# A two-layer graph network, last stage: five of nine chunks get relu and residual by VectorE out of PSUM

## What is computed

```python
h = maximum(layernorm(x), 0)
x = x + relu(gcn(h, W, b, gamma, beta, src, dst))       # first layer: scatter over the edges
h = maximum(layernorm(x), 0)
agg = segment_sum(edge_attr, dst)                       # sums of edge attributes by node
m = relu(concat([h, agg, u]) @ W1 + b1)
m = relu(m @ W2 + b2)
out = x + m @ W3 + b3
```

## Time and profile before

| | us |
|---|---|
| median of 3 runs | 744.41 |
| the 3 runs | 744.41, 748.85, 740.71 |
| the profiled execution: time | 737.08 |
| the profiled execution: span of the rows | 735.3 |
| TensorE busy | 669.1 (91%) |
| VectorE busy | 569.5 (77%) |
| ScalarE busy | 456.4 (62%) |
| GpSimd busy | 147.9 (20%) |

### The profile page before, as it was taken

The page is one execution under the profiler, slowest core; times in us unless marked ns, Lnnn a source line. Parts: engine busy times, 40 slices in busy tenths (PEclk is TensorE's granted clock), DMA queues, the critical chain, the costliest instruction groups (busy, mean ns, idle before and its releaser), DMA issues. The chain is left out here.

```text
span 735.3 us, 21540 instructions
## 1 busy us (share of the span) xinstructions
PE 669.1 (91%) x9010; PEld 574.0 (78%) x9010; DVE 569.5 (77%) x1115; ACT 456.4 (62%) x811; POOL 147.9 (20%) x184
## 2 busy tenths in 40 slices
PE   0898764899999999999999999989999999998996
PEld 0766553688988888888888988979888888896554
DVE  5997985988888888888888888488888898845622
ACT  1563583666666666667766666376666766666862
POOL 3652851111111110111111111020000000003622
PEclk9997685999999999999999999999999999999999
DMA  6300710556555444445555555365555555660122
GB/s 154 115 1 3 260 38 2 216 216 216 216 216 203 178 180 176 177 174 199 214 214 214 214 214 195 140 219 210 177 180 182 208 214 214 214 171 5 42 59 76
DMA packets 64878, 119.75 MB, mean 163 GB/s; under 512 B 3077, under 2 KB 22739, under 8 KB 64807
## 3 DMA queue, kind: packets, MB, share of 16 engines
q1 hardware_dynamic: 64246, 117.89, 45.7%
q0 software_dynamic: 576, 1.12, 0.6%
HBM read 115.81 MB, written 4.03 MB: 163 GB/s over the span
## 5 line engine op out<-in xcount | busy, mean ns | idle before, releaser
L1562 PE MATMUL ps_product<-counts_sb,table_sb 128*128 128x240 f16 (+1 forms) x2646 | 408.7, 261 | 0.0
L1381 ACT CAST counts_sb<-ps_counts 128x588 f16<-128x588 f32 x524 | 335.9, 649 | 103.5 <-PE ps_counts L1552 59.3
L1552 PE MATMUL ps_counts<-key_hot,lo_hot 128*128 128x147 bf16 x2096 | 384.9, 232 | 15.1 <-DVE key_hot L1430 6.2
L1562 PEld LDWEIGHTS ps_product<-counts_sb,table_sb 128*128 128x128 f16 x2646 | 240.4, 97 | 8.1
L1552 PEld LDWEIGHTS ps_counts<-key_hot,lo_hot 128*128 128x128 bf16 x2096 | 198.2, 98 | 60.1 <-ACT counts_sb L1381 17.8
L1430 DVE TENSOR_TENSOR key_hot<-key,iota_key 128x1176 bf16<-128x1176 f16 x262 | 199.7, 762 | 0.0
L1425 DVE TENSOR_TENSOR lo_hot<-src_lo,iota_key 128x1024 bf16<-128x1024 f16 x262 | 180.8, 690 | 17.7 <-PE ps_counts L1552 12.6
L1365 POOL TENSOR_SCALAR place_hot<-iota_c,slot_now 128x96 f32<-128x96 f32 x81 | 60.3, 757 | 470.6 <-PE ps_place L1598 457.1
L1441 DVE TENSOR_TENSOR attr_hot<-rel,iota_w 128x640 f32<-128x640 int16 x81 | 66.9, 825 | 54.9 <-PE ps_sums L1572 54.9
L1572 PE MATMUL ps_sums<-attr,attr_hot 128*32 128x128 f32 x3240 | 95.6, 276 | 0.0
L1572 PEld LDWEIGHTS ps_sums<-attr,attr_hot 128*32 128x32 f32 x3240 | 88.1, 111 | 4.5 <-issue 4.1
(11 more groups left out here) (279 smaller groups left out, 536.3 us busy)
## 6 DMA issues: line engine op xcount, KB each, us to landing
attr<-in_edge_attr_dram SPq DMA_DIRECT2D x80, 1280.0 KB, 8.2
acc<-in_x_dram SPq DMA_DIRECT2D x4, 768.0 KB, 8.5
attr<-in_x_dram SPq DMA_DIRECT2D x12, 256.0 KB, 5.3
out_dram<-y_ring SPq DMA_DIRECT2D x12, 256.0 KB, 2.3
src_padded<-in_src_dram SPq DMA_DIRECT2D x1, 805.7 KB, 7.4
attr<-in_edge_attr_dram SPq DMA_DIRECT2D x2, 320.0 KB, 8.0
attr<-in_edge_attr_dram SPq DMA_DIRECT2D x1, 640.0 KB, 3.9
raw_d<-in_dst_dram SPq DMA_DIRECT2D x1, 540.0 KB
```

What stands on the lines that cost most here:

```text
L1381: act.copy(counts_sb[s % 2][:].rearrange("p h (n t) -> p h n t", n=WN) [:, :, :, k * QUAD:(k + 1) * QUAD], ps_counts[n % 2][:, :, 0:KEYS]. ...
L1552: ins = pe.matmul(ps_counts[quad % 2][:, c, 0:KEYS], lo_hot[:, held, pair, :, q % 2], key_hot[:, held, pair, :, q % 2], start=True, stop=True)
L1562: ins = pe.matmul(ps_product[side][:, 0:SLOTS] if tiles == TS else product, table_sb[:, h, low, :], counts_sb[side][:, h, :] if tiles == T ...
```

## The change

For the later chunks with an even number (4, 6, 8, 10 and 12) VectorE does, in a new function `join`, what ScalarE and GpSimd did: for each block one `scalar_tensor_tensor` out of `ps_turn[0]`, `dinv * sums + x` into `relu_ring[0]`, then, after waiting for the last of them, one `tensor_tensor` over the chunk that takes the maximum of that and `x`, into `xs`. That is relu and residual at once, as max(a + x, x) = relu(a) + x. `join(c)` stands in VectorE's slot of `TURNED_IN`, behind the copy h2t and ahead of the statistics of the slot before. The wait of chunk 12 for its loaded rows (`tail_in`) goes with it to VectorE.

The odd chunks (5, 7, 9 and 11) stay with ScalarE and GpSimd. They alone use `ps_turn[1]` and `relu_ring[1]` now, and the even ones bank and slot 0. So `turn_sums` waits for `joined` ahead of chunks 6, 8, 10 and 12, and for `relu_ready` ahead of 7, 9 and 11; the statistics and x3 of an even chunk wait for `joined` (`x1_is_ready`). Nothing else is changed, and the DMAs are the same.

```diff
--- before.py
+++ after.py
@@ -1680,16 +1680,23 @@
             ps_turn, ps_h2, ps_3 = ([bank(f"ps_{n}{k}", [P, NC], scope) for k in range(2)] for n in ("t", "h", "three"))
             ps_1, ps_2 = (bank(f"ps_{n}", [P, NC], scope) for n in ("one", "two"))
             (zeroed, b1u_done, b1u_ok, conv_turned, relu_ready, x1_ready, dve_step, var_ok, root_ok, norm_ok, h2_ready,
-             h2_turned, h2t_ready, m1_ready, z1_ready, m2_ready, z2_ready, m3_ready, x3_ready, y_ready, tail_in) = (
+             h2_turned, h2t_ready, m1_ready, z1_ready, m2_ready, z2_ready, m3_ready, x3_ready, y_ready, tail_in, joined) = (
                 sem(f"mlp_{n}", scope) for n in
                 "zeroed b1u_done b1u_ok conv_turned relu_ready x1_ready dve_step var_ok root_ok norm_ok h2_ready "
-                "h2_turned h2t_ready m1_ready z1_ready m2_ready z2_ready m3_ready x3_ready y_ready tail_in".split())
+                "h2_turned h2t_ready m1_ready z1_ready m2_ready z2_ready m3_ready x3_ready y_ready tail_in joined".split())
             y_out = [sem(f"y_out{k}", scope) for k in range(2)]
 
             def slot(buffers, c):
                 return buffers[:, c % 2, 0:width(c) * P]
 
 
+            def x1_is_ready(engine, c):
+                if c % 2:
+                    engine.wait_ge(x1_ready, (c - LEAD) // 2 + 1)
+                else:
+                    engine.wait_ge(joined, (c - LEAD) // 2 + 1)
+
+            assert LEAD % 2 == 0
             TURNED_IN = {0: range(4, 6), 1: range(6, 8), 2: range(8, 10), 3: range(10, 12), 4: range(12, CHUNKS)}
             MEASURED_IN = {2: 1, 5: 2}
             NORMAL_IN = {3: 1, 6: 2}
@@ -1717,9 +1724,9 @@
                     pool.memset(xs[:, FB, :], 0.0).then_inc(zeroed, 1)
                     for s in SLOTS_ALL:
                         for c in TURNED_IN.get(s, ()):
-                            if c == CHUNKS - 1:
-                                pool.wait_ge(tail_in, 16)
-                            pool.wait_ge(relu_ready, c + 1 - LEAD)
+                            if c % 2 == 0:
+                                continue
+                            pool.wait_ge(relu_ready, (c - LEAD) // 2 + 1)
                             pool.tensor_tensor(chunk(xs, c), chunk(xs, c), slot(relu_ring, c), ALU.add)\
                                 .then_inc(x1_ready, 1)
                         if M3_AT <= s < CHUNKS + M3_AT:
@@ -1727,7 +1734,7 @@
                             if c == 0:
                                 pool.wait_ge(mlp_in, 16 * MLP_LOADS)
                             if c >= LEAD:
-                                pool.wait_ge(x1_ready, c + 1 - LEAD)
+                                x1_is_ready(pool, c)
                             if c >= 2:
                                 pool.wait_ge(y_ready, c - 1)
                             pool.tensor_tensor(slot(x3_ring, c).rearrange("p (b f) -> p b f", b=width(c)),
@@ -1740,8 +1747,20 @@
                     link = chained(v, dve_step)
 
                     def take_stats(c):
-                        v.wait_ge(x1_ready, c + 1 - LEAD)
+                        x1_is_ready(v, c)
                         return take_block_stats(v, c)
+
+                    def join(c):
+                        v.wait_ge(conv_turned, c + 1 - LEAD)
+                        if c == CHUNKS - 1:
+                            v.wait_ge(tail_in, 16)
+                        for k in range(width(c)):
+                            n = c * BC + k
+                            part = slice(k * P, (k + 1) * P)
+                            ins = v.scalar_tensor_tensor(out=relu_ring[:, 0, part], in0=ps_turn[0][:, part],
+                                                         scalar=dinv[:, n:n + 1], in1=xs[:, n, :], op0=ALU.mult, op1=ALU.add)
+                        link(ins)
+                        v.tensor_tensor(chunk(xs, c), chunk(xs, c), slot(relu_ring, c), ALU.max).then_inc(joined, 1)
 
                     v.wait_ge(b1u_done, 1)
                     v.tensor_tensor(b1u[:], ps_3[0][:, 0:1], B1, ALU.add).then_inc(b1u_ok, 1)
@@ -1762,6 +1781,9 @@
                             if s >= 2:
                                 v.wait_ge(m1_ready, s - 1)
                             v.tensor_copy(slot(h2t_ring, s), ps_h2[s % 2][:, 0:width(s) * P]).then_inc(h2t_ready, 1)
+                        for c in TURNED_IN.get(s, ()):
+                            if c % 2 == 0:
+                                join(c)
                         if s >= 1:
                             for c in TURNED_IN.get(s - 1, ()):
                                 ins = take_stats(c)
@@ -1774,7 +1796,7 @@
                     def take_relu(c):
                         act.wait_ge(conv_turned, c + 1 - LEAD)
                         if c >= LEAD + 2:
-                            act.wait_ge(x1_ready, c - 1 - LEAD)
+                            act.wait_ge(x1_ready, (c - LEAD) // 2)
                         for k in range(width(c)):
                             n = c * BC + k
                             part = slice(k * P, (k + 1) * P)
@@ -1811,13 +1833,17 @@
                         if 2 <= s + 1 < CHUNKS:
                             normalize(s + 1)
                         for c in TURNED_IN.get(s, ()):
-                            take_relu(c)
+                            if c % 2:
+                                take_relu(c)
 
                 @block.tensor
                 def _(pe):
                     def turn_sums(c):
                         if c >= LEAD + 2:
-                            pe.wait_ge(relu_ready, c - 1 - LEAD)
+                            if c % 2:
+                                pe.wait_ge(relu_ready, (c - LEAD) // 2)
+                            else:
+                                pe.wait_ge(joined, (c - LEAD) // 2)
                         for k in range(width(c)):
                             b = c * BC + k
                             ins = pe.transpose(ps_turn[c % 2][:, k * P:(k + 1) * P], acc[:, 0, b * P:(b + 1) * P], ident[:])
```

## The result

Over 20 runs each the changed kernel took 744.68 us (742.41 to 750.48) and the kernel before 740.80 us (739.33 to 748.85). The ratio is 1.006, with a 95% interval of 1.0038 to 1.0082: slower by 0.4 to 0.8%, so within the 1% that the prediction set, in the range, and on the side that it named. But 3.1 us (the difference of the fastest runs) to 4.4 us (by the ratio; 2.8 to 6.1 by its interval) is two to nearly three times the 1.6 us of its sum.

A forecast was written before the change was run, and what follows sets the result against it. It took TensorE to bound the last stage's steady slots; M2(0) at -0.9, M2(1) +1.1, M2(2) +0.7, M2(4) +1.5 and the end +1.6 us gave 744.41 + 1.6 = 746.0 us. The range was 740.5 to 751 us.

The forecast's parts named there:

- its sum: Last stage: gains and delays passed through the engine queues put the end of the kernel 1.6 us later.
- What bounds the stage: Last stage: TensorE alone bounds the steady slots at 4.26 us each; the change only moves when they begin.
- Prices: VectorE's joins: products 0.26 us from start to start (bounds 0.20 and 0.34), a 512-column maximum 0.67 us.
- The gain: Slots 1 and 2: ScalarE, with fewer relus, starts z1(0) sooner, so M2(0) comes 0.9 us earlier.
- The loss at the first root: Slot 2: joins delay VectorE's variances by 2.1 us, so the root is late and M2(1) starts 1.1 us later.
- The recovery ahead of M2(2): Slot 3: TensorE's little wait for ScalarE disappears, so the lag falls from 1.1 to 0.7 us.
- The second root: Slots 5 and 6: join(12) and a POOL collision delay the variances; the lag grows by 0.8 us at M2(4).
- PE runs nearly without a gap in either kernel: Slots 3 and 4: TensorE works on almost without waiting; only the wait ahead of M2(2) goes, leaving 0.7 us lag.
- The four large maxima: VectorE's 512-column maxima each start before the GpSimd add they could collide with, by margins of 0.25 to 0.7 us.
- case C: Rival, chance 0.20: a maximum waits for POOL's add, with slower products; +3.7, up to 5.5 us: 747.4 to 750.
- The small one of chunk 12: join(12) ahead of the second root: its maximum alone is caught by a POOL instruction, for 0.6 us.
- A: Forecast case, chance 0.55: VectorE is late at the two roots; +0.5 to +3 us, 744.9 to 747.4.

The follow-up runs named there:

- filler3: Changed kernel with three unused 512-column matmuls on TensorE ahead of the wait of M2(1): stage 67.50 us, whole time 1.0019 of the kernel before.
- product_psum: Changed kernel with the join's products written in place into PSUM, so the maximum reads PSUM and SBUF: stage 68.50 us.
- filler1: Changed kernel with one unused 512-column matmul on TensorE ahead of the wait of M2(1): stage 69.02 us.
- only_4_6_8: Changed kernel with only chunks 4, 6 and 8 joined by VectorE, 10 and 12 left with ScalarE and GpSimd: stage 68.62 us.
- joins_last: Changed kernel with each join moved behind the statistics and variances of its slot: stage 68.04 us, whole time 1.0061 of the kernel before.
- before_lag4: Kernel before, without the change, plus 16 unused VectorE statistics instructions ahead of those of slot 2: stage 69.50 us.
- before_lag6: Kernel before, without the change, plus 24 unused VectorE statistics instructions ahead of those of slot 2: stage 70.91 us.

## Why the prediction was right, and where its sum was short

**What bounds the stage: right.** The steady slots are the same as in the earlier trace rows: in the chain of the changed kernel one M2 starts at 706.41 and the next at 710.68 us, 4.27 us later. The change moved only their beginning.

**Prices: right.** Products 1.12 us for four, maximum 0.69 us. None of the bounds on them was needed.

**The gain: right.** M2(0) 0.71 us earlier, where the text had 0.9; ScalarE was idle ahead of z1(0).

**The loss at the first root: right in kind, 0.5 us too small.** The variances ended 2.5 us late instead of 2.1, M2(1) came 1.57 us late instead of 1.1. M2(0) was 0.2 us later than in my schedule, and between its start and the first transpose of chunk 8 lay 0.96 us, where I had let the queue go on sooner; VectorE stood idle for 0.50 us ahead of join(8).

**The recovery ahead of M2(2): wrong.** I took 0.4 us off, as a wait for ScalarE that would go. The row of that M2 in the earlier trace rows shows no idle time, so I had misread it. In every kernel at full clock M2(1) to M2(2) is 5.13 or 5.14 us; it was no wait. The lag stays: filler3 has +1.58 at M2(1) and at M2(2).

**The second root: right in kind, too large.** It was late and cost 0.43 us (filler3: +1.59 us at M2(3), +2.02 at M2(4)), where I had 0.8. The queues alone come to +2.06 us, as filler3 shows, against my 1.6.

**The step that fell short** is the sentence that behind M2(1) "PE runs nearly without a gap in either kernel": it priced TensorE's work there at its rate before, after a wait that my own schedule had made more than 3 us long. The clock was not in the sum, not among the rivals, and not in the list of what would prove me wrong. It is 1.43 us, the largest term after the lag itself. The sum should have been 2.06 + 1.43 = 3.49 us.

The Trainium skill (TensorE: Matmul & The Clock Gate, section "What's actually happening") describes an idle TensorE as falling back to its half-rate level of 1.2 GHz; the trace agrees, with 0.50 and 0.53 in these stretches. It was the rule to weigh here, and I had looked only at the one on VectorE and GpSimd. Idle time isn't the only thing that comes before a fall in these traces, though: far ahead of this stage, in the kernel before, the clock was 1.00 between 64 and 65 us, 0.83 in the next microsecond and 0.50 from 66 to 70 us, with TensorE busy for all of these 6 us.

**VectorE and GpSimd.** The four large maxima came first, as forecast, by 0.34 to 0.65 us; case C did not happen. The small one of chunk 12 was caught for 0.63 us (0.92, and 0.29 in product_psum), where the text had 0.6. POOL waited for a maximum in its turn, which the rows of before couldn't show, and less than the 0.4 us that the text allowed: add(5) took 1.50 us, and 1.27 once the maximum reads PSUM; add(9) took 1.32 us, and add(11) its usual 1.27. The rule of the Trainium skill (SBUF — State Buffer, section "SBUF: two separate sides") that the lock works in both directions is borne out.

**Cases.** A was the right mechanism, but at +3.49 us in the stage it lies beyond A's own range of 3, in numbers that I had given to C. The range held because C was there, not because C was right. The measured 744.68 us as such says little: the forecast of 746.0 was counted from a median of 744.41, and over 20 runs that kernel's median is 740.80, so an anchor that was 3.6 us too high more than made up for the 2.3 us (3.9 by the medians, less 1.6) that the sum lacked. Counted from 740.80, the sum gives 742.4, A 741.3 to 743.8 and C 743.8 to 746.4, and the measured time lies in C's numbers again. That it came so close to 746.0 is luck.

**Still open:** whether anything in the early stages adds to the 3.49 us of the stage, which lie within the interval of the ratio (2.8 to 6.1 us). And why the clock falls right at the end of the idle time in four kernels (the changed one, filler1, product_psum, only_4_6_8), and a microsecond or more after work has been taken up again in joins_last and before_lag4. In before_lag6 it fell 1.5 us before the end of the idle time.

## What to carry to other kernels

Moving work from a busy engine to an idle one is worth what the receiving engine's next deadline leaves it: find the first signal that it has to give behind the new work (here the variances, 0.9 us ahead of need), and place the work behind that. When a schedule worked out makes TensorE wait, price what follows at the lower clock as well: 2.3 to 3.5 us of waiting cost another 1.4 to 1.7 us here, 4.0 us cost 2.65 us, and 1.1 us cost nothing. On VectorE, keep a PSUM operand in two-input instructions that run beside GpSimd.

## What the runs showed of the hardware that I had not expected

- In this stage the granted clock fell to half with 2.26, 2.54, 3.40, 3.41, 3.53 and 3.96 us of TensorE idle time, in each kernel that had so much, and in none where the longest was 1.43 us. M2(1) to M2(2) then took 6.61 to 7.78 us instead of 5.13.
- In joins_last the fall came when TensorE had been at work again for one microsecond, so the matmul right behind a wait can look healthy (1.14 us) and the next ones not (1.91 us for eight transposes instead of 1.04).
- Extra matmuls without any use made the stage 1.43 us shorter.
- A VectorE instruction of 0.17 to 0.19 us with two SBUF inputs took 1.25 and 1.29 us beside GpSimd adds of 512 columns; with one input in PSUM the collision was gone (0.29 us instead of 0.92 for the small maximum).
